# A two-layer graph kernel: the first count before the support's products, transposes before weighing, packs one tick sooner

## The reference

```python
# x (2048, 64), adj (2048, 2048) of 0 and 1, all float32
# layer 0
support = x @ w0
rank = cumsum(adj != 0, axis=1);  deg = rank[:, -1:];  k = minimum(deg, 100)
pos = rank - (deg - k)
w = mask * where(pos > 0, 0.5 ** (k - pos), 0.0)
x = layernorm(x + w @ support + b0)
# layer 1
deg = clip(sum(adj, axis=1) + 1, 1)
z = concatenate([x, (adj @ x + x) / deg]) @ w1 + b1
out = relu(z);  out = out / maximum(norm(out), 1e-12)
x = layernorm(x + out)
```

## Time and profile before

| | us |
|---|---|
| median of 3 runs | 110.85 (110.51 to 111.42) |
| the profiled execution's own time | 110.75 |
| its span in the profile | 108.8 |
| TensorE busy with products | 92.6 (85%) |
| VectorE busy | 63.4 (58%) |
| ScalarE busy | 57.4 (53%) |
| share of TensorE in the chain that ended last | 65% |
| mean granted clock of TensorE | 0.974 of full |

### The profile page before, as it was taken

One profiled execution on the slowest core, in us unless ns is written; L12 is line 12 of the kernel. 1 busy time (PEld: TensorE's weight loads), 2 busy tenths in 40 slices (PEclk: granted clock), 3 DMA queues, 4 the chain that ended last, 5 costly groups with the idle time before them and its releaser, 6 DMA issues.

```text
span 108.8 us, 2398 instructions
## 1 busy us (share of the span) xinstructions
PE 92.6 (85%) x886; PEld 72.4 (67%) x886; DVE 63.4 (58%) x188; ACT 57.4 (53%) x125; POOL 18.8 (17%) x44
## 2 busy tenths in 40 slices
PE   5938789999999999999996799999999999995000
PEld 2326448677778777776764477779989999994000
DVE  2224632352862424389799934148983339999991
ACT  0503866453766565756577486783032208478740
POOL 6200000000000009000009500000000000467860
PEclk9999999999999999999999999999999999999955
DMA  2999999999979999996979970000000000000124
GB/s 52 315 339 358 349 321 350 385 387 389 383 234 399 388 387 386 386 386 236 193 141 121 202 136 0 6 0 0 0 6 0 0 0 6 0 0 12 36 54 94
DMA packets 23867, 20.23 MB, mean 186 GB/s; under 512 B 13617, under 2 KB 17713, under 8 KB 23857
## 3 DMA queue, kind: packets, MB, share of 16 engines
q1 hardware_dynamic: 23696, 20.06, 60.4%
q10 hardware_dynamic: 160, 0.03, 0.1%
HBM read 17.47 MB, written 0.52 MB: 165 GB/s over the span
## 4 chain that ended last, share of the span: by engine, by line
PE 65%; DVE 17%; DMA 11%; issue 3%; ACT 1%; ACTq 1%; DVEq 0%
PE acc L878 17%; PE cnt L865 10%; PE cnt L867 10%; PE tmp L846 9%; PE acc L909 7%; DMA adjT<-nat 6%; DMA wd<-in_L_gnn_weight_dram 5%; PE cnt L909 5%; PE tmp L897 3%; DVE stats L447 3%; DVE t L582 3%; DVE adjT L545 2%; DVE t L593 1%; PE acc L923 1%; PE tmp L923 1%
## 5 line engine op out<-in xcount | busy, mean ns | idle before, releaser
L330 ACT ACTIVATE wts<-cnt 128x512 int16<-128x512 f32 x64 | 37.8, 596 | 20.4 <-PE cnt L867 20.1
L878 PEld LDWEIGHTS acc<-sup,wts 128*128 128x128 bf16 x256 | 22.8, 98 | 13.7 <-issue 0.5
L878 PE MATMUL acc<-sup,wts 128*128 128x192 bf16 x256 | 30.8, 246 | 0.0
L545 DVE COPY adjT<-tmp 128x1024 bf16<-128x1024 bf16 x24 | 16.4, 688 | 20.3 <-PE tmp L846 20.3
L865 PE MATMUL cnt<-adjT,rest 128*128 128x512 bf16 x60 | 22.7, 379 | 3.7 <-DMA adjT<-nat 1.6
L867 PE MATMUL cnt<-adjT,suffix 128*128 128x512 bf16 x64 | 24.2, 379 | 0.0
L285 POOL TENSOR_TENSOR adjT<-adjT,ident 128x128 bf16<-128x128 bf16 x16 | 7.3, 492 | 50.4 <-PE cnt L867 50.4
L846 PE MATMUL tmp<-ident,stage 128*128 128x128 bf16 x192 | 14.5, 219 | 0.7 <-DMA stage<-in_adj_dram 0.7
L846 PEld LDWEIGHTS tmp<-ident,stage 128*128 128x128 bf16 x192 | 12.3, 98 | 1.8 <-issue 1.2
L909 PE MATMUL acc<-ysp,adjT 128*128 128x194 bf16 x128 | 11.8, 247 | 0.0
L909 PEld LDWEIGHTS acc<-ysp,adjT 128*128 128x128 bf16 x128 | 10.8, 98 | 0.3
(11 more groups left out here) (101 smaller groups left out, 85.3 us busy)
## 6 DMA issues: line engine op xcount, KB each, us to landing
stage<-in_adj_dram SPq DMA_DIRECT2D x12, 1024.0 KB, 13.3
stage<-in_adj_dram SPq DMA_DIRECT2D x8, 512.0 KB, 8.0
xs<-in_x_dram SPq DMA_DIRECT2D x2, 256.0 KB, 6.0
out_dram<-xs SPq DMA_DIRECT2D x3, 128.0 KB, 2.0
out_dram<-xs SPq DMA_DIRECT2D x2, 64.0 KB, 1.7
wd<-in_L_gnn_W_dram SPq DMA_DIRECT2D x4, 16.0 KB, 7.9
adjT<-nat SPq DMA_TRANSPOSE x4, 5.0
wd<-in_L_gnn_weight_dram ACTq DMA_DIRECT2D x2, 16.0 KB, 4.8
```

Source lines behind the costliest of these rows:

```text
L330: nc.scalar.activation(wts[:, c, n % WRING, :].bitcast(I16), cnt[:, c, :], ACT.Relu).then_inc(w_ready[c], 1)
L545: nc.vector.tensor_copy(adjT[:, q, bp // 2, :, bp % 2 * 2:bp % 2 * 2 + 2, :], bank.bitcast(BF16).rearrange("p (r k n) -> p r k n", r=RT, k ...
L878: last = nc.tensor.matmul(acc[:, c * RT + r, 0:PD], wts[:, c, n % WRING, r * P:(r + 1) * P], sup[:, b, :], start=(b == NB - 1 and r % 2 == ...
```

## The change

TensorE counts the first block and transposes the second stream's first pair before the products of the support. Within a tick the fills stand in front of `weigh` of stream 0. ScalarE makes the high part of the support after the first weights instead of before, and the middle part two ticks later; VectorE's two steps of the split move back by one m. All packs come one m sooner. The bias is added at m = 17 and no longer at m = 24. Behind the loop the sum of group 3 out of `acc` comes after the layer norm's part 4 of group 2.

```diff
-PIECES = {20: ((0, 0), (0, 1)), 21: ((0, 2), (0, 3)), 22: ((1, 0), (1, 1)), 23: ((1, 2), (1, 3)),
-          24: ((2, 0), (2, 1), (2, 2), (2, 3)), 25: ((3, 0), (3, 1)), 26: ((3, 2), (3, 3))}
+PIECES = {19: ((0, 0), (0, 1)), 20: ((0, 2), (0, 3)), 21: ((1, 0), (1, 1)), 22: ((1, 2), (1, 3)),
+          23: ((2, 0), (2, 1), (2, 2), (2, 3)), 24: ((3, 0), (3, 1)), 25: ((3, 2), (3, 3))}
...
-            act.wait_ge(sup_done, 1)
-            nc.scalar.activation(sup[:, PT:NB, 0:D], ..., ACT.Copy, scale=SUP_SCALE).then_inc(sup_hi, 1)
...
                 if tick == 0:
+                    act.wait_ge(sup_done, 1)
+                    nc.scalar.activation(sup[:, PT:NB, 0:D], ..., ACT.Copy, scale=SUP_SCALE).then_inc(sup_hi, 1)
+                if tick == 2:
                     act.wait_ge(sup_left, 1)
                     nc.scalar.copy(sup[:, PT:NB, D:2 * D], left32[:, PT:NB, :]).then_inc(sup_mid, 1)
...
             for m in range(MARKS):
-                if m == 2:
+                if m == 3:
                     dve.wait_ge(sup_hi, 1)
...
-                if m == 3:
+                if m == 4:
                     dve.wait_ge(sup_mid, 1)
...
-                if m == ENDS[0] + 4:
+                if m == ENDS[0] - 3:
                     dve.wait_ge(par_loaded, 16 * 6)
...
-            for q, part in ((2, 0), (2, 1), (2, 2), (2, 3), (3, 0), (2, 4), (3, 1), (3, 2), (3, 3), (3, 4), (2, 6), (2, 7),
+            for q, part in ((2, 0), (2, 1), (2, 2), (2, 3), (2, 4), (3, 0), (3, 1), (3, 2), (3, 3), (3, 4), (2, 6), (2, 7),
...
             transpose_adj(0)
+            pe.wait_ge(consts, 6)
+            count(0, 0)
+            transpose_adj(1)
             pe.wait_ge(w0_loaded, 32)
             pe.wait_ge(xT_ready, 1)
             support(1, acc_bank(6)).then_inc(sup_done, 1)
-            pe.wait_ge(consts, 6)
...
-            filled = 1
+            filled = 2
             for tick in range(TICKS):
-                if tick < STEPS:
+                if 0 < tick < STEPS:
                     count(0, tick)
-                if LAG <= tick:
-                    weigh(0, tick - LAG)
                 while filled <= tick + (1 if tick + 1 < FOLLOW else LEAD):
                     fill(filled)
                     filled += 1
+                if LAG <= tick:
+                    weigh(0, tick - LAG)
```

More of the change, by code:

```diff
@@ L316, in _ @@
             nc.scalar.activation(root[:, 0, 0:1], square[:, 0:1], ACT.Sqrt)
-            act.wait_ge(sup_done, 1)
-            nc.scalar.activation(sup[:, PT:NB, 0:D], acc[:, 6:8, :].rearrange("p a (b d) -> p (a b) d", d=D),
-                                 ACT.Copy, scale=SUP_SCALE).then_inc(sup_hi, 1)
             def spread_root0(q):
@@ L351, in _ @@
                 if tick == 0:
+                    act.wait_ge(sup_done, 1)
+                    nc.scalar.activation(sup[:, PT:NB, 0:D], acc[:, 6:8, :].rearrange("p a (b d) -> p (a b) d", d=D),
+                                         ACT.Copy, scale=SUP_SCALE).then_inc(sup_hi, 1)
+                if tick == 2:
                     act.wait_ge(sup_left, 1)
```

## The result

The changed kernel takes 109.45 us (109.13 to 109.77, 4 runs) against 110.94 beside it: a ratio of 0.9886, 95% interval 0.9852 to 0.992. That is 1.1% faster by the ratio, 1.3 us, and inside the forecast range; the time lies a microsecond above the 108.5 that was forecast. A second measurement of the same kernel gave 0.9892 (0.9857 to 0.9927). Executions more than 1.5% above the same kernel's fastest are left out of the ratios, but not of the medians, and a profile taken in one isn't read.

What follows compares the result with a forecast made beforehand. TensorE was taken to bound the kernel, leaving the chain at the start, copy waits and DMA transpose XB; `count(1, 24)` at 58.2 instead of 60.55 saves 2.3 us, 110.75 to 108.45, called 108.5; range 107.7 to 110.1.

Steps and rivals of the forecast that it cites:

- XA: DMA transpose of unit A: issued at 48.3, held behind D's load, landing at 55.1 as before, soon enough for `count(0, 24)`.
- XB: DMA transpose of unit B, before `count(1, 24)`: issue 0.85 us sooner, landing at 58.0, just in time for TensorE at 58.2.
- the third rival: Start and tick order give little: count under 0.6 us ahead at tick 19, time 108.9 to 109.5; chance 0.09.
- The start: First counts of the kernel: first count near 7.8 instead of 8.85, fifth count about 1.05 us sooner.
- The order in a tick: Early ticks: waits for copies at ticks 6 and 8 go; count 1.7 us ahead by tick 10.
- Ticks 19 and 20: VectorE's packs wait for A's load, delaying sums; TensorE stalls 0.6 us, and only 0.6 of the 1.7 comes through.
- the mis-sized term: Time from D's landing to XA's landing, taken as 1.8 us.
- signs of being wrong: A's or D's landing moved over 0.5; XA landing at 53; XB wait over 1 us; new wait behind 62 us.
- the first rival: XB stays slow: 6.1 us from its issue, landing at 59.6; 0.85 us gained, time 109.9; chance 0.28.
- Behind it: After `count(1, 24)`: TensorE's 30 us and the tail follow unchanged, so its 2.3 us gain is kept.

Runs made afterwards that it cites:

- XA in front of D's load: Full change, with SyncE issuing the DMA transpose of unit A before the load of the last unit, D: 1.0113, 112.09 us, against the kernel before.
- the order in a tick alone: Kernel before with only the transposes put in front of weighing in each tick: 0.9881, 109.44 us.
- packs alone: Kernel before with only VectorE's packs moved one m sooner: 0.9959, 110.07 us.
- all but packs: Full change with the packs left where they were in the kernel before: 0.9892, 109.8 us.
- full change: All edits of the change together, against the kernel before: 0.9886, 109.45 us.
- full change again: The full change measured a second time, unaltered, against the kernel before: 0.9892.
- sums first: Full change with A's packs at m = 20 and 21 and all four of B at m = 22, behind the sums: 0.9845, 109.53 us.
- ticks old: Full change with weighing again in front of the transposes in each tick; start and packs stay: 0.9912, 109.75 us.
- D by ScalarE: Full change with D's load issued from ScalarE's queue at tick 19, not SyncE's; run twice: 0.9836, 109.28 us, and 0.985, 109.43 us.
- D by ScalarE, sums first: Full change with D's load issued by ScalarE and the packs of A and B behind the sums: 0.9934, 110.15 us.
- small loads by ScalarE: Full change with six loads of biases and second weights issued by ScalarE at the start, not SyncE in the middle: 0.9969.
- small loads by ScalarE, sums first: Full change with the six small loads issued by ScalarE at the start and the pack table of sums first: 0.9926.

## Why the prediction was right, and where it was off

The profiles of all kernels but the one with XA in front of D's load, in us (D, XA, XB: landings; for the order in a tick alone there is none that can be read):

| kernel | D | XA | XB | resume | TensorE waited for |
|---|---|---|---|---|---|
| before | 53.3 | 55.1 | 60.4 | 60.55 | XB |
| packs alone | 53.1 | 55.0 | 59.0 | 59.15 | XB, little |
| all but packs | 54.3 | 57.6 | 59.1 | 60.0 | XA |
| full change | 53.9 | 56.5 | 58.2 | 58.99 | XA |
| full change again | 52.7 | 55.3 | 58.9 | 58.97 | XB |
| sums first | 53.7 | 57.0 | 58.6 | 59.4 | XA |
| ticks old | 54.5 | 57.2 | 58.8 | 59.6 | XA, little |
| D by ScalarE | 53.5 | 56.8 | 58.4 | 59.3 | XA |
| D by ScalarE, sums first | 54.8 | 56.5 | 60.7 | 60.9 | XA and XB |
| small loads by ScalarE | 54.6 | 58.6 | 60.3 | 61.1 | XA, little |
| small loads by ScalarE, sums first | 53.5 | 56.8 | 58.5 | 59.3 | neither |

The forecast was a gain of 2.35 us, and 1.56 came. Its mechanism held: TensorE's lead and XB's sooner issue, the lead shortened at ticks 19 and 20, XA's issue held until D's landing. The time, 109.45, lies outside the 0.4 that the forecast gave itself around 108.5. It lies where the third rival had put it (108.9 to 109.5), whose condition didn't come true: the count at tick 19 was 1.24 us ahead (47.39 to 46.15), not under 0.6.

*The start.* Forecast 1.05 sooner at the first count, measured 0.57 (8.28), and 0.5 to 1.15 in seven other profiles with the same start (7.70 to 8.36). The landing of the first half unit varies (5.5 to 6.7 us), but isn't all: with D by ScalarE it landed at 5.52 and the transposes began at 6.52, behind the products of `warm`. A sooner first count also bought nothing: in the sums-first profile it came at 7.70, but the second transposes waited for their load until 8.46, and the fifth count (15.14) and `count(0, 10)` (28.83) stood where the full change's do (15.17, 28.86).

*The order in a tick.* The waits for copies went. The fifth count was 0.60 ahead, not 1.05, and `count(0, 10)` 1.23 (30.09 to 28.86), not 1.7: between the two the change gained the 0.6 that was forecast, and the shortfall of the start was carried along.

*Ticks 19 and 20.* The wait of VectorE for A was there (0.73). But A landed at 44.9, 0.5 sooner than taken, and TensorE came to the first weighing of group 2 at 47.03, when the sum had been over since 46.55: the first of the two stalls, forecast at 0.6, was zero. The second was 0.51, and the first weighing of group 3 started at 50.44 against 50.6 forecast. Of the lead there remained 0.73 us. That this came out within 0.2 is partly luck. The forecast said that VectorE has no gap behind A's landing; it had one of 0.24, for B, which landed at 48.64. From A's landing to the weighing it was 5.5 us against the 5.14 worked out, and A's sooner landing made up for it. Where B didn't hold VectorE the sum of 5.14 was right: 5.2 with D by ScalarE (45.1 to 50.29) and with XA in front of D's load (45.4 to 50.64).

*XA.* The step that failed is "it lands at 55.1, no sooner than before. That is soon enough". It landed at 56.5 and cost 0.93 of TensorE. That the issue would be held until D's landing was right. Of the 1.4 us that XA came later than taken, 0.6 are D's own landing (53.9 against 53.3), and 0.8 are the mis-sized term, what comes behind that landing. I took 1.8 us from the one row there was; the profiles in the table give 1.8 to 4.0. The price is 0.8 of the 2.3 forecast: 58.2 became 58.99. The forecast's own signs of being wrong included a landing of A or D moved by over 0.5; D's moved by 0.6.

*XB.* Taken at 58.0, measured 58.2: right by luck. It was taken 2.9 us behind an XA at 55.1, and came 1.6 behind one at 56.5. In the repeated measurement it took 6.3 us and was the one that held TensorE, so the first rival (XB stays slow) happened too, half as dear as priced.

*Behind it* everything followed unchanged, as forecast: 1.56 at the resume, 1.6 in the span.

What the forecast didn't see is that the parts of the change don't add up. Packs alone give 0.4%, the order in a tick 1.2%, start and order 1.1%, start and packs 0.9%, all of it 1.1%; the start alone, and order with packs, were not run. In every profile but that of small loads by ScalarE with the sums first TensorE waits for XA or XB, and it resumes 5.1 to 6.4 us behind D in every row of the table but the one of the kernel before, where it was 7.2 because XB's packs came 1 us behind D. So most of the parts bring TensorE or XB's issue up to the same point, the last load's landing plus two DMA transposes. How far this goes is not shown in full. The point isn't sharp: the two profiles of the full change alone stand 5.1 and 6.3 us behind D, a difference nearly as large as the change's gain. In that one exception TensorE was itself late and waited for neither. And for the order in a tick alone it is argued only. What makes D land sooner was not found, and no kernel here is clearly faster than the full change.

The Trainium skill's rule that I had weighed against the change (DMA: Bandwidth & Descriptors, Queues, rings and completion order: descriptors are taken in ring order on each engine) gives the right outcome for XA behind D in one queue, but isn't the whole reason: with D in another queue nothing changed. By the same page's section Issuing engines are not separate DMA queues, DMAs from all engines run on the same 16 engines and interleave. The trace agrees in so far as the other queue brought nothing: XA's 8.8 us with D on ScalarE's queue equal the 8.7 with D on SyncE's. It doesn't show XA's packets interleaved with D's: XA was issued at 48.03, and landed 3.3 us behind D (53.5).

## What to carry to other kernels

Before pulling a step forward, ask which event it will then wait for. Here two edits each brought their engine to a DMA transpose that hangs on the last load, and the second edit to get there earned nothing that the intervals could tell. Undo each part alone as well as doing it alone: the order in a tick was worth 1.2% by itself and 0.2% in company, and only both numbers show that the bound had moved.

## What the runs showed of the hardware

A DMA transpose of 0.5 MB that was issued while loads were pending, on its own queue or on another, kept its issue busy until about the landing of the last of them (2.9 to 6.6 us, ending within 0.4 of that landing), and landed 1.7 to 4.0 us behind it. Behind transposes alone an issue took 1.4 to 4.5 us, and the longest looked alike: XD's in the full change, 4.45 us, ended at 62.8, with XC's landing at 62.3. A transpose behind a transpose landed 1.5 to 5.3 us later. Where XA landed less than 2 us behind D, XB needed 4.1 to 5.3 more; where XA was slower XB mostly needed 1.6 to 1.8 (3.5 in the repeated measurement), and why is open. Six loads of 16 and 32 KB, issued beside the matrix's loads at the start, took the rate of the DMA engines down to 208 GB/s for a slice of 2.7 us; in the middle the slice was at 234 and 293, so that moving them only moved the dip.

Twice a wait at TensorE cost more than its length. With XA in front of D's load, and with the small loads issued by ScalarE, the granted clock fell from 1.00 to 0.5 (1.2 GHz) for some 3 us, behind stretches in which TensorE had been busy for 0.5 of 3 us and for 2.1 of 4. Behind the waits for XB in the kernel before (1.59) and with D by ScalarE and the sums first (1.76) it stayed at 1.00.
